# Dense one-hots of a graph kernel: batches of eight slots instead of four, in the same sixteen slots

## The reference

```
src_h = h[src] @ W_msg.T + b_msg
msg = src_h + edge_embed[edge_type]                 # 9 types
messages = segment_sum(msg, dst, num_segments=12500)
gi = messages @ W_ih.T + b_ih
gh = h @ W_hh.T + b_hh
r = sigmoid(i_r + h_r); z = sigmoid(i_z + h_z)
n = tanh(i_n + r * h_n)
h_new = (1 - z) * n + z * h
out = layernorm(x + h_new)
```

## Time and profile before

| | us |
|---|---|
| median of 3 runs | 1080.8 (1079.31 to 1081.71) |
| the profiled execution | 1078.91 |
| its span (first to last instruction) | 1077.1 |
| PE busy | 990.0 |
| DVE busy | 854.2 |
| POOL busy | 733.5 |
| ACT busy | 667.3 |
| chain that ended last | PE 74%, DVE 9%, ACT 7%, issue 5% |

### The profile page before, as it was taken

One profiled execution on the slowest core, in us unless ns is written; L12 is line 12 of the kernel. 1 busy time (PEld: TensorE's weight loads), 2 busy tenths in 40 slices (PEclk: granted clock), 3 DMA queues, 4 the chain that ended last, 5 costly groups with the idle time before them and its releaser, 6 DMA issues.

```text
span 1077.1 us, 23527 instructions
## 1 busy us (share of the span) xinstructions
PE 990.0 (92%) x8411; PEld 651.6 (60%) x8411; DVE 854.2 (79%) x2699; ACT 667.3 (62%) x1283; POOL 733.5 (68%) x779
## 2 busy tenths in 40 slices
PE   6779899999999999999999999999999999999983
PEld 2256655666566666666666666666666666666652
DVE  8747797887878978878988887878887888898544
ACT  5655156566766657677666666667676667666522
POOL 7777777766676766767666676666676767677740
PEclk9876899999999999999999999999999999999996
DMA  8887223333333333333333333333333334343331
GB/s 267 230 270 252 53 66 95 93 86 86 89 85 100 90 89 89 97 83 91 100 89 97 84 94 88 96 91 93 94 100 96 104 87 109 90 104 103 94 91 27
DMA packets 94565, 114.23 MB, mean 106 GB/s; under 512 B 19820, under 2 KB 80616, under 8 KB 94441
## 3 DMA queue, kind: packets, MB, share of 16 engines
q0 software_dynamic: 35264, 73.19, 25.4%
q1 hardware_dynamic: 57320, 37.79, 11.9%
q10 hardware_dynamic: 1856, 1.66, 0.5%
HBM read 96.56 MB, written 16.00 MB: 105 GB/s over the span
## 4 chain that ended last, share of the span: by engine, by line
PE 74%; DVE 9%; ACT 7%; issue 5%; POOL 2%; DMA 2%; SPq 1%; DVEq 0%; ACTq 0%
PE psf L1097 36%; PE psb L1082 14%; PE psg L1065 6%; PE pAB L1026 6%; PE pAB L1040 6%; ACT mem L1213 3%; PE psg L1069 2%; PE pAB L1043 2%; DVE ohk L665 1%; PE psg L1061 1%; POOL xg L604 1%; DVE ohl L868 1%; DVE ohk L862 1%; PE psf L1108 1%; DVE ohk L865 1%
## 5 line engine op out<-in xcount | busy, mean ns | idle before, releaser
L604 POOL DMA_INDIRECT xg<-x_split,idx x648 | 614.9, 949 | 270.6 <-issue 170.7
L1097 PE MATMUL psf<-mem 128*128 128x384 bf16 (+1 forms) x2744 | 606.2, 327 | 12.1 <-ACT arena L1223 9.3
L1213 ACT CAST mem<-psb 128x432 f16<-128x432 f32 x896 | 435.1, 523 | 249.8 <-PE psb L1082 245.9
L1082 PE MATMUL psb<-ohk,ohl 128*128 128x108 bf16 (+3 forms) x1865 | 411.4, 261 | 15.8 <-ACT mem L1213 10.6
L862 DVE TENSOR_TENSOR ohk<-table_bank,prm 128x392 bf16<-128x392 f16 (+3 forms) x437 | 270.9, 620 | 77.8 <-PE psb L1082 74.1
L1097 PEld LDWEIGHTS psf<-mem 128*128 128x128 f16 (+1 forms) x2744 | 238.3, 98 | 129.7 <-issue 23.1
L1082 PEld LDWEIGHTS psb<-ohk,ohl 128*128 128x128 bf16 x1865 | 172.2, 99 | 137.4 <-issue 19.9
L868 DVE TENSOR_TENSOR ohl<-table_bank,prm 128x512 bf16<-128x512 f16 x437 | 180.9, 414 | 0.0
L865 DVE TENSOR_TENSOR ohk<-table_bank,sort 128x40 bf16<-128x40 f16 (+3 forms) x437 | 106.6, 244 | 0.0
L604 POOL DMA_INDIRECT xg<-in_x,idx x88 | 85.0, 965 | 27.3 <-issue 24.4
L891 DVE TENSOR_TENSOR mem<-mem,psg 128x136 f32 (+9 forms) x184 | 54.4, 296 | 55.8 <-PE psg L1069 54.8
(11 more groups left out here) (148 smaller groups left out, 804.5 us busy)
## 6 DMA issues: line engine op xcount, KB each, us to landing
xg<-x_split,idx POOLq DMA_INDIRECT x648
x_split<-mem SPq DMA_DIRECT2D x24, 384.0 KB
xb<-in_xT SPq DMA_DIRECT2D x49, 128.0 KB, 3.0
arena<-in_x SPq DMA_DIRECT2D x24, 256.0 KB, 5.1
arena<-in_xN SPq DMA_DIRECT2D x47, 128.0 KB
out<-spill SPq DMA_DIRECT2D x19, 128.0 KB
out<-arena SPq DMA_DIRECT2D x144, 8.0 KB
out<-arena SPq DMA_DIRECT2D x15, 128.0 KB
```

Of the source, the lines that this page charges most:

```text
L604: pool.indirect_dma_start(out=xg[:, p % RING, :] if split else xg32(p % RING), out_offset=None, in_=x_d if split else x, in_offset=bass.In ...
L1082: ins = pe.matmul(psb[:, bank % NB, held * HC:(held + m) * HC], ohl[:, e % KB, :], ohk[:, e % KB, d * HC:(d + m) * HC], start=(k == 0), st ...
L1097: pe.matmul(psf[:, 0:3 * H], Bb[q % 2][0:kk, HT + h, :], xs[0:kk, h, :, :].rearrange("p c f -> p (c f)"), start=(h == 0), stop=(h == HI - ...
L1213: act.copy(Bb[q % 2][:, :, n:n + MOST], psb[:, bank % NB, 0:MOST * HC].rearrange("p (d h) -> p h d", h=HC)).then_inc(S["s_eb"], 1)
```

## The change

Two constants: a batch has eight slots, and the sixteen slots of buffers hold two batches.

```
-OB = 4
-KB = 4 * OB
+OB = 8
+KB = 2 * OB
```

## The result

The changed kernel takes 1109.4 us (median of 4 runs, 1108.25 to 1110.52), the kernel before 1080.2 us in the same series; the ratio is 1.0272 with a 95% interval of 1.026 to 1.0284. It is slower by 29 us, where the prediction said 17. The profiled execution has a span of 1106.7 us against 1077.1.

The account below looks back on a forecast made before the run. PE (TensorE) was taken as the bound, DVE as having slack. Terms: reserve 18, sum at L903 +3, clock +2, absorbed -6, together +17 us on the median 1080.8: 1098 us; eight-in-ten range 1079 to 1118.

Parts of the forecast that it names:

- The direction and the mechanism: Whole kernel: slower, because the change lightens DVE, which isn't the bound, and shortens the reserve, so PE waits for one-hots.
- DVE's saving: One-hot operations on DVE: 654 fewer save 43 us, padding adds 20, net 23; by the record some 74 us less.
- The reserve, 18 us: One-hots made 8 slots ahead instead of 12: late batches make PE wait 18 us in 21 stretches; bounds 0 and 48.
- the comparison: For all 217 batches, DVE's old start plus the batch-of-eight price against PE's first matmul; largest lateness per stretch, 24 us.
- The named ones: New or existing waits named beforehand: near slot 904, at 113.80 us (3.93 us already), and slots 1592 on.
- The place worked out: Slots 888 to 904: DVE, level with PE at 510.77, readies slot 904's batch at 520.6; PE waits 1.85 us.
- The clock, +2: TensorE's granted clock: 21 new waits may bring one half-speed drop, half of 3.4 us: +2 (0 to +8).
- The sum at L903, +3: DVE's sum behind longer batches: some 6 us more in seven places, 3 won in five; +3 (-4 to +9).
- Absorbed, -6: PE's existing 32 us of idle time swallows a third of the 18 us of new waits: -6 (0 to -12).
- the rival of waits that feed on each other: PE and DVE stop each other, the clock halves, late finals hold the next block: some 45 us, 1126; chance 0.08.

Follow-up runs that it names:

- The two runs with a heavier DVE: Kernel before with batches of four padded to the widest of eight slots: 1081.4 us; kernel before with eight batches of two: 1080.5 us.
- exact signals: Changed kernel with a PE signal after every eighth slot, so DVE never waits for a later slot than needed: 1092.9 us, ratio 1.0117.
- both repairs: Changed kernel with a PE signal after every eighth slot and each batch of eight made as two sets of four, each signalled: 1089.5 us, ratio 1.0084.
- three batches of four, rare signals: Kernel before with three batches of four, PE signalling after eight slots without a finished bank instead of four: 1097.5 us, ratio 1.0166.

## Why the prediction was right, and what was mis-sized

**The direction and the mechanism held.** The change relieves an engine that isn't the bound, and the new time is PE waiting. The two runs with a heavier DVE show the first half, since 18 us of more DVE time moved the kernel by 0.15% (at most 0.27% by the interval) and 71 us, with two more slots in hand, by 0.04%. The profile after shows the second.

**DVE's saving.** By the records L862, L865 and L868 take 256.4 + 77.8 + 148.5 = 482.7 us, against 558.4; 76 less where 74 was said. The page's busy time falls by 17.9 us, near the net 23 from start to start.

**The reserve, 18 us.** The size came near: waits of PE for one-hots rose by 14.8 us in its own row and 21.5 in that of the weight loads. In the weight loads' row 21 waits from 104 us on are over 0.45 us, 5 before; the comparison said 21 new stretches. The named ones are among them: slot 904 (1.31 us in PE's row), slot 1592 (0.50) and slot 72, where the wait only grew from 3.93 to 4.44. But the reason inside the term was mis-sized, and that the sum of the waits came near is luck. The comparison gave the late signals 2 of 23 us (so the expectation of the run with a signal after every eighth slot says) and the shorter, coarser reserve the rest. The runs put it the other way: with those signals 17 of 29 us are gone. The step that failed is the comparison itself. It took DVE's start from the trace of before, where DVE waits for late signals too (102 of 433, by one to three slots, not by one or two), and so carried that lateness over to a version without them. The place worked out has it: the start at 510.77 is the end of a wait of 2.03 us for the signal of slot 882, which PE reached at 510.52, while the buffers were free after slot 879, at 508.02. With exact signals PE waits there for 0.28 us, not for 1.31. That the comparison counted each late batch only against its own slot, and not for what the held DVE does late afterwards, is a second gap; how much it hid is not shown.

**The clock, +2.** It was 5 to 8. PE is busy for 8.6 us more with the same instructions. From the first slot product to the last PE is busy for 897.1 us against 889.1, and the granted clock was at half for 40 us in all, against 29. The 11 us more cost half of that, 5 to 6 us; the rest of the 8.6 isn't traced. The prediction had one new drop, and the bound that it gave, 8 us, was nearly what came: beyond the start, which runs at half up to 100 us in both, there are six stretches of 3.4 us in place of one of 6.8 and one of 3.4. One of them, at the end of a block in the changed kernel, stands behind a wait for the sum:

```profile
559.20 0.49 PE L1108 MATMUL psf<-ident,added 128*128 128x128 f32 x2 [2.05 <-DVE added L903]
...
561.70 0.89 PE L1065 MATMUL psg<-ohs,xg 128*128 128x68 bf16 x12
```

Before it, the same twelve products of L1065 take 0.54 us:

```profile
554.19 0.54 PE L1065 MATMUL psg<-ohs,xg 128*128 128x68 bf16 x12
```

The busy time of that stretch (last three columns: granted clock, DMA, GB/s) reads:

```profile
560.60:564.00 3.40, 3.40 (x25) 2.31 (x24) 2.14 (x5) 1.80 (x2) 0.91 (x1) 0.50 0.10 27
```

**The sum at L903, +3.** It was 2.6 in PE's row.

**Absorbed, -6.** It was not there; this term and the clock are why the forecast was 12 us short. The old waits didn't swallow the new ones but grew themselves: ACT's copies by 4.0, the copy behind the sum by 2.0, and only 2.4 went elsewhere. With the measured terms the prediction's sum reads 14.8 (one-hots) + 2.6 (sum) + 8.6 (busy, mostly the clock) + 4.0 + 2.0 (ACT's copies) - 2.4 = 29.6 us. That ACT's waits grew because DVE's finals came later, and ACT waits for them in its own order, is argued from the order and not shown by a run. Against the forecast the terms are off by -3.2, -0.4, +6.6 and +9.6, together 12.6 us. The measured time so lies on the side of the rival of waits that feed on each other: the clock at its bound and the old waits longer, though far from that rival's 1126.

**The Trainium skill.** The rule for an engine that isn't saturated but makes others wait (Perfetto Trace Analysis, Optimizing Scalar/DVE Operations) gave the right sign: grouping cost 29 us here, and breaking the batches of eight up again won 5 or 6 us. It won them only with a signal for each half; with one signal for both the same operations cost 8 us. At the full reserve, where there was little left to win, batches of two gained nothing.

**What stays open.** With both repairs 9 us (0.84%) remain against the kernel before. 5 of them are the shorter reserve, as the run with three batches of four has them. The other 4 would be the lumps in DVE's order, for which the longer waits for the sum speak (15.8 to 20.6 us), but no run took the lumps away alone. A batch of eight at the full reserve, with more buffers, was not tried.

## What to carry to other kernels

When two constants trade the size of a batch against the number of batches in the same buffers, price the reserve and not the operations: on an engine with idle time a saved operation is worth next to nothing as long as the reserve holds, and the reserve has an edge (12 slots: 0, 8 slots: 5 us, 4 slots: 90 us). Look at what else hangs on the same constant. Here it also set how often the consumer signals, and that was more than half of the loss; a consumer should signal exactly where the producer looks. And where a critical engine waits for one operation in a producer's fixed order, move the filler behind it: that, with the signals, gave 0.7%. Read the busy time of the bound too, and over several executions: part of a loss by waits shows up there.

## What the runs showed of the hardware

The clock of TensorE can amplify waits: in the changed kernel six separate stretches of 3.4 us between 116 and 840 us were granted half speed, in the kernel before one of 6.8 and one of 3.4. Five of the six begin within 1.5 us of the end of a PE wait of 2.0 to 4.4 us, the sixth behind waits of 1.3 and 1.8 us; other waits of 1.1 to 1.8 us had no such stretch behind them. From the first to the last slot product of each profiled execution (us):

| kernel | PE idle | PE busy | clock at half |
|---|---|---|---|
| before | 40.5 | 889.1 | 29 |
| three batches of four | 45.7 | 888.4 | 24 |
| changed, signal after every eighth slot | 52.2 | 891.0 | 34 |
| three batches of four, rare signals | 53.0 | 895.6 | 34 |
| changed | 63.2 | 897.1 | 40 |
| two batches of four | 105.0 | 922.1 | 65 |

The same products take up to 33 us more where PE waits 65 us more. It doesn't follow the waits closely when they are few: 5 us more of idle time cost nothing with three batches of four. And it differs between executions of one kernel: in one series the kernel before took 1076.2 to 1083.7 us, with a mean granted clock of 0.971 in the shortest and 0.960 in the longest. A few us of busy time between two single profiles can therefore be this scatter and not the order's work.
